# The second batch's layer norm placed ahead of GpSimd's masking in the second cross-attention, its query four units later, and zero products in TensorE's gaps

## What is computed

```
x = x + L0_xattn(layernorm(x), ctx)        # 16 heads of 64, softmax over 2048 keys
x = x + L0_attn(layernorm(x))              # latent attention with rope, causal, 16 heads of 8
x = x + L0_ffn(layernorm(x))               # 8 experts, the best one taken, gelu
x = x + L1_xattn(layernorm(x), ctx, mask)  # second cross-attention, 16 heads of 8
x = x + L1_attn(layernorm(x))              # one head of 128
x = x + L1_ffn(layernorm(x))               # 16 experts, 8 taken, and a shared one

L1_xattn: scores = (x Wq)(ctx Wk)^T / sqrt(8);  masked keys -> -1e32
          t = relu(scores + nbias)^2;  attn = t / (sum(t) + 1e-32);  (attn V) Wo
```

## Time and profile before

| | busy us | share of the span |
|---|---|---|
| TensorE (PE) | 430.9 | 89% |
| VectorE (DVE) | 343.6 | 71% |
| ScalarE (ACT) | 274.3 | 57% |
| GpSimd (POOL) | 165.3 | 34% |

### The profile page before, as it was taken

The page is one execution under the profiler, slowest core; times in us unless marked ns, Lnnn a source line. Parts: engine busy times, 40 slices in busy tenths (PEclk is TensorE's granted clock), DMA queues, the critical chain, the costliest instruction groups (busy, mean ns, idle before and its releaser), DMA issues.

```text
span 485.0 us, 8723 instructions
## 1 busy us (share of the span) xinstructions
PE 430.9 (89%) x3404; PEld 359.3 (74%) x3404; DVE 343.6 (71%) x538; ACT 274.3 (57%) x432; POOL 165.3 (34%) x108
## 2 busy tenths in 40 slices
PE   5897999999899999999878888699949999985896
PEld 3575899999799999999877745466437888864685
DVE  3478778878877888878631484761888999974574
ACT  2256667667567866667650235421019999982344
POOL 0012532334433633332536047300052657430024
PEclk9699899999899999999999899799959999999899
DMA  7613235332233323334359300089750000010000
GB/s 258 230 28 93 54 84 165 87 76 71 55 77 88 87 67 88 76 77 119 76 160 431 150 0 2 0 173 216 161 246 2 3 3 3 2 31 0 2 0 12
DMA packets 26984, 43.07 MB, mean 89 GB/s; under 512 B 5952, under 2 KB 24128, under 8 KB 25280
## 3 DMA queue, kind: packets, MB, share of 16 engines
q1 hardware_dynamic: 26944, 42.52, 31.3%
HBM read 19.30 MB, written 0.13 MB: 40 GB/s over the span
## 4 chain that ended last, share of the span: by engine, by line
PE 67%; DVE 15%; ACT 7%; issue 5%; SPq 2%; DMA 2%; POOL 1%; POOLq 0%; ACTq 0%; DVEq 0%
PE ps L561 6%; PE ps L563 6%; PE ps L562 6%; PE ps L583 5%; PE ps L585 5%; PE ps L584 5%; PE ps L577 5%; PE ps L832 4%; PE ps L855 3%; PE ps L932 3%; PE ps L789 3%; PE ps L797 3%; DVE max L1385 3%; DVE w_ring L1543 2%; SPq L449 2%
## 5 line engine op out<-in xcount | busy, mean ns | idle before, releaser
L1247 POOL TENSOR_TENSOR dT_lo<-z_sq,dT_hi 128x1024 fp32r<-128x1024 f32 x32 | 76.3, 2386 | 120.3 <-ACT dT_hi L961 120.3
L1385 DVE TENSOR_REDUCE max<-ps 128x1 f32<-128x1024 f32 x64 | 78.2, 1222 | 17.6 <-PE ps L563 14.5
L1543 DVE SCALAR_TENSOR_TENSOR w_ring<-ps,neg_nbias,cap 128x1024 f32<-128x1024 f32 x56 | 67.7, 1277 | 3.8 <-PE ps L832 3.3
L961 ACT ACTIVATE eT_hi<-ps 128x512 fp32r<-128x512 f32 x64 | 38.2, 597 | 54.4 <-PE ps L577 54.4
L561 PE MATMUL ps<-ctxT_hi,qk_hi 128*128 128x512 f32 x128 | 54.3, 425 | 8.7 <-ACT p_d L1030 7.3
L1180 ACT ACTIVATE p_ring<-w_ring,nbias_sb 128x1024 f32<-128x1024 f32 x56 | 61.6, 1145 | 0.6
L1372 DVE TENSOR_TENSOR eT_lo<-ps,eT_hi 128x512 fp32r<-128x512 f32 x64 | 43.9, 686 | 20.0 <-ACT eT_hi L961 19.9
L563 PE MATMUL ps<-ctxT_lo,qk_hi 128*128 128x512 f32 x128 | 52.4, 410 | 0.0
L562 PE MATMUL ps<-ctxT_hi,qk_lo 128*128 128x512 f32 x128 | 52.3, 409 | 0.0
L1381 DVE STREAM_TRANSPOSE y_sq<-p_d 128x1024 f32<-128x1024 f32 x32 | 39.9, 1245 | 16.8 <-ACT p_d L1030 15.9
L1030 ACT ACTIVATE p_d<-ps,nmax 128x1024 f32<-128x1024 f32 x32 | 35.7, 1115 | 27.2 <-DVE nmax L1415 27.2
(11 more groups left out here) (217 smaller groups left out, 891.9 us busy)
## 6 DMA issues: line engine op xcount, KB each, us to landing
z_sq<-y_sq SPq DMA_DIRECT2D x256, 64.0 KB, 2.1
w_sb<-in_w SPq DMA_DIRECT2D x2, 2048.0 KB, 14.4
kstack<-k_hi SPq DMA_DIRECT2D x8, 512.0 KB, 10.0
ctxT_raw<-in_ctx_t SPq DMA_DIRECT2D x2, 1024.0 KB, 7.3
ctx_raw<-in_ctx_nat SPq DMA_DIRECT2D x2, 1024.0 KB, 8.7
ctxT_raw<-in_ctx_t SPq DMA_DIRECT2D x1, 2048.0 KB, 7.7
kstack<-k_lo SPq DMA_DIRECT2D x4, 512.0 KB, 10.6
wg_sb<-in_wg SPq DMA_DIRECT2D x1, 1088.0 KB, 5.1
```

What stands on the lines that cost most here:

```text
L961: return nc.scalar.activation(dst, src, ACT.Copy)
L1247: nc.gpsimd.tensor_tensor(d_ring(dT_lo, m), z_chunk(m), d_ring(dT_hi, m), ALU.subtract)\
L1385: return v.tensor_reduce(max2[:, p:p + 1], ps[:, 2 * p:2 * p + 2, :], AX.XY, ALU.max)
L1543: v.scalar_tensor_tensor(w_ring[:, (at - 1) % 3, :].rearrange("p (h n) -> p h n", h=4), ps[:, bank:bank + 2, :].rearrange("p a (h n) -> p ...
```

## The change

Three things change.

1. Zero products are added: 4 ahead of `turn_xn(1)`, 2 inside it (between its transposes and its wait for the copy), 2 behind the latent product, 12 ahead of `turn_xn(2)`, 2 inside it, 4 behind `make_q1(0)`, and 6 behind the scores of units 2 and 3, where a wait for the copies of the first query stands ahead of them (they write its bank, 7).
2. `turn_xn(3)` moves from behind the last product of L797 to the middle of its last group of four. The first query goes to two banks (its first group to bank 3, the others to bank 7, by `q1_bank`), ScalarE copies the first group and signals it before the others are copied, and VectorE splits and spreads the first group as soon as it is there. `make_q1(0)` waits for `acc_zero`, since bank 7 is cleared by VectorE.
3. GpSimd waits for `xn_ready` of `layer_norm(4)` ahead of its loop. `turn_xn(4)` moves from m = 0 to m = 4 on TensorE, `make_q1(1)` from m = 2 to m = 6, ScalarE's copies likewise from m = 0 to m = 4 and m = 6 (each ahead of that unit's square), and VectorE's split of the second query from m = 4 to m = 9.

```diff
+        def q1_bank(b, g):
+            return 3 if b == 0 and g == 0 else 7
...
-            def turn_xn(i):
+            def turn_xn(i, bank=None):
                 pe.wait_ge(xn_ready, i + 1)
                 for b in range(*NORMS[i]):
                     last = nc.tensor.transpose(ps[:, XT_BANK[i], b * S:(b + 1) * S], xn[:, b, :], ident[:])
                 last.then_inc(xnT_psum, 1)
+                if bank is not None:
+                    keep_warm(bank, 2)
                 pe.wait_ge(xnT_ready, i + 1)
...
             fill(0)
-            turn_xn(1)
+            keep_warm(4, 4)
+            turn_xn(1, 4)
             pe.wait_ge(load["small"], 16 * N_SMALL)
             mm(ps[:, 5, T:2 * T], w_lat[:], xnT[:], start=True, stop=True).then_inc(lat_psum, 1)
+            keep_warm(4, 2)
...
             fill(3)
-            turn_xn(2)
+            keep_warm(4, 12)
+            turn_xn(2, 4)
...
                     for f in range(NF):
+                        if b and eh and f == NF // 2:
+                            turn_xn(3)
...
                 for g in range(4):
-                    last = mm(ps[:, 7 * b, g * S:(g + 1) * S], wq1[:, g, :], xnT[:, b * S:(b + 1) * S],
+                    last = mm(ps[:, q1_bank(b, g), g * S:(g + 1) * S], wq1[:, g, :], xnT[:, b * S:(b + 1) * S],
                               start=True, stop=True)
-                last.then_inc(q1_psum, 1)
+                    if g == 0 and b == 0 or g == 3:
+                        last.then_inc(q1_psum, 1)
             pe.wait_ge(load["wq1"], 16)
-            turn_xn(3)
+            pe.wait_ge(acc_zero, 1)
             make_q1(0)
+            keep_warm(2, 4)
...
                 if u == 1 and c == 1:
-                    pe.wait_ge(q1_done, 4)
+                    pe.wait_ge(q1_done, 6)
...
-                if m == 0:
+                if m == 2:
+                    pe.wait_ge(q1_done, 4)
+                    keep_warm(7, 6)
+                if m == 4:
                     turn_xn(4)
-                if m == 2:
+                if m == 6:
                     make_q1(1)
...
-            def copy_q1(b):
-                act.wait_ge(q1_psum, b + 1)
+            def copy_q1(b, g0_, g1_):
                 for t in (q1s, q1):
-                    nc.scalar.activation(t[:, :, b * S:(b + 1) * S], ps[:, 7 * b, :].rearrange("p (g s) -> p g s", g=4),
+                    nc.scalar.activation(t[:, g0_:g1_, b * S:(b + 1) * S],
+                                         ps[:, q1_bank(b, g0_), g0_ * S:g1_ * S].rearrange("p (g s) -> p g s", s=S),
                                          ACT.Copy, scale=SCALE1).then_inc(q1_done, 1)
-            copy_q1(0)
+            act.wait_ge(q1_psum, 1)
+            copy_q1(0, 0, 1)
+            act.wait_ge(q1_psum, 2)
+            copy_q1(0, 1, 4)
...
                     relu_first(0)
-                    copy_xnT(4)
-                    copy_q1(1)
...
+                if m == 4:
+                    copy_xnT(4)
+                if m == 6:
+                    act.wait_ge(q1_psum, 3)
+                    copy_q1(1, 0, 4)
...
             pool.wait_ge(keep_done, 1)
+            pool.wait_ge(xn_ready, 5)
...
             spread_q(v, 0).then_inc(qbd_done, 1)
+            dve.wait_ge(q1_done, 4)
             split_q1(0, slice(1, 4))
             layer_norm(4)
...
-                if m == UNITS // 2:
-                    dve.wait_ge(q1_done, 4)
+                if m == UNITS + 1:
+                    dve.wait_ge(q1_done, 6)
                     split_q1(1, slice(0, 4))
```

More of the change, by code:

```diff
@@ L508, in _, with keep_warm @@
             mm = nc.tensor.matmul
-            def turn_xn(i):
+            def keep_warm(bank, count):
+                for _ in range(count):
+                    mm(ps[:, bank, 0:T], zeros[:, 0:P], zeros[:], start=True, stop=True)
+            def turn_xn(i, bank=None):
                 pe.wait_ge(xn_ready, i + 1)
@@ L515, in turn_xn @@
                 last.then_inc(xnT_psum, 1)
+                if bank is not None:
+                    keep_warm(bank, 2)
                 pe.wait_ge(xnT_ready, i + 1)
-            def keep_warm(bank, count):
-                for _ in range(count):
-                    mm(ps[:, bank, 0:T], zeros[:, 0:P], zeros[:], start=True, stop=True)
             pe.wait_ge(warm, 1)
```

## The result

The changed kernel takes 485.56 us (median of 4 runs, 484.38 to 487.33) against 491.88 for the kernel before, measured beside it: ratio 0.9882, 95% interval 0.9835 to 0.9928. Two later measurements, each beside the kernel before, gave 0.9879 (0.9821 to 0.9938) and 0.9906 (0.9865 to 0.9946). The forecast was 488.1 us, a gain of 4.3 us. The profiled executions are closer together than the medians: 484.83 against 486.96 us. Each ratio is taken from fast runs alone: executions over 1.5% above the fastest of their kernel are left out of it.

The account below looks back on a forecast made before the run. Three engines are full at once in the second cross-attention's loop, so only its beginning has slack. The terms -0.5 + 0.8 - 4.6 (the last including 0.1 lost) gave -4.3, from 492.38 to 488.1 us, range 485.3 to 490.8.

Parts of the forecast that it names:

- A: Start of the latent attention: with zero products its instructions run at full clock and end at 277.2, 0.5 us gained.
- B: Twelve zero products ahead of `turn_xn(2)`: they outlast the norm, the transposes start at 311.0, 0.8 us lost.
- the lower bound (+0.3): Ahead of the experts: if the first `diag` takes its undisturbed 1.2 us, L780 starts at 316.0, 0.3 us late.
- C: The first query, around `turn_xn(3)`: scores start at 353.25 against 353.13, 0.1 us lost (bounds 0.4 gained, 0.6 lost).
- D: Start of the second cross-attention's loop: undisturbed `layer_norm(4)` and later second query bring combination 1's relu 4.6 us earlier.
- rival 1: Clock falls inside TensorE's new wait in `turn_xn(4)`: 489.7 us, chance 0.18; if it lasts until 367, 491.8 us.
- Catching up (2): In the loop, the shifted start removes the 0.3 us waits, up to 2.1 us more gained: 486.0 us, chance 0.08.
- The slow twelve (3): The twelve products ahead of `turn_xn(2)` run at half clock, experts start some 9 us late: 496 us; slower cases 0.08.
- Rival 4: `layer_norm(4)` is slowed by something other than GpSimd: about 1 us gained, 491.8 us; chance 0.13 together with a long fall.

Follow-up runs that it names:

- e3: The changed kernel without any of its added zero products, moves and GpSimd's wait kept: 486.52 us, ratio 0.9954 to the kernel before.
- e4: The changed kernel without its early zero products, those of the second cross-attention kept: 486.60 us, ratio 0.9943; again 485.56 us, 0.9891.
- the wait alone: The kernel before with GpSimd's wait for the norm as its only edit: 486.08 us, ratio 0.9940; again 486.11 us, 0.9903.

## Why the prediction was right

**What bounds.** Right. Three engines are full in the loop, and u to z is 62.59 to 63.10 in every profile of the table: the start of the loop alone moved its end.

**A.** 0.5 gained by forecast, 0.68 measured. In two later profiles without early zero products the half-clock stretch was missing all the same: there s to r is 8.89, and against those A loses 1.0. **B.** 0.8 lost, 0.72 measured. The transposes start at 311.00, the number forecast (`fill(3)` ended within 0.1 us of where it did before). The first `diag` started ahead of `k_lo`, so the lower bound (+0.3) applied to the first selection, 315.89 against 315.67. The other one came later by more. A and B cancel: s to e is 53.09 with them, 53.05 before, and 53.06 and 52.99 in the profiles of e3 and e4. In the second profiles of the wait alone and of e4 it is 53.52 and 53.58, so there the early products would be worth 0.5. What the forecast did not price is a smaller number of products: seven, with none inside `turn_xn(2)`, gain 1.15 us over none (41.32 against 42.47).

**C.** 0.1 forecast, 0.35 measured, within its bounds. Too small in it was the stop in the last group: VectorE's last part came 0.82 us later relative to the first expert product (351.02 - 321.08 against 349.38 - 320.26), not 0.57, and its splitting of the query starts right behind it, long after the early copy is there.

**D.** 4.6 forecast with C's 0.1 in it, so 4.7 from the first scores to the end of the loop; 3.6 measured (81.33 to 77.76). Of the four terms it is the furthest off. The walk was right to 0.3 us up to TensorE's wait (first `w_ring` 3.25 after the scores against 3.35, the wait 1.68 against 1.75), and there rival 1 came true: the clock was half from 363.2 to 366.6, which the prediction had also named as a sign of being wrong (half clock behind 360). Its price was 1.5 us (13.46 against 14.99), 1.6 in the rival. Without the fall D is 5.1, 0.4 over the forecast. Of the three profiles of the changed kernel the clock fell in two, and of all six with this loop in four; what decides it isn't shown. The Trainium skill, TensorE: Matmul & The Clock Gate, section Why this matters for your kernels, asks that gaps stay under about 3 us. That was not enough here: the gap was 1.7 us.

The forecast tied D too closely to the clock: with TensorE at half clock as before it left 1 us of gain. The wait alone, at half clock for 10 us, gained 3.5 us of q to u, and for 17 us still 1.55. The falls in the kernel before were also read late: by the earlier trace rows they came at 308.1 and 352.4, not at 308.5 and 352.7, so the idling ahead of the second was 1.7 us.

**The sum.** In the profiled executions the gain is 2.1 us: the stages s to z give 3.2, and 0.8 was lost ahead of s and 0.2 behind z, in code that did not change. In the runs the ratios of the three measurements come to 5.8, 6.0 and 4.6 us (each times the median of before, as 0.0118 x 491.88). So the size forecast, 4.3, is a little low against the runs and high against the first profile. The mechanism was right; that the number came out inside the range is in part luck. Taken from 492.38, the stages' 3.2 us would give 489.2 us, near what rival 1 said (489.7). The 485.56 measured lies below that and only 0.3 us above the lower end of the range. No stage explains it; the third measurement, with the most runs of before, is closest to the stages. What in the executions of before adds the difference in the other two is open.

**Rivals.** Catching up (2) did not happen: a combination takes 8.78 us (relu to relu, mean of six) against 8.76, and the waits of 0.2 to 0.4 us are all there. The slow twelve (3) did not: by the microsecond view the clock was full from 269 to 347. Rival 4 is refuted by the norm's 2.87 us.

## What to carry to other kernels

Where a stage has three full engines, as this loop has, look at its first few microseconds for what stands ahead of the bottleneck's first instruction in its own program order: there was all that this change could win. Keep a chain of small VectorE instructions clear of long GpSimd ones with SBUF inputs; one wait on the engine with slack was, by the medians, the whole gain. Size zero products to end with what TensorE waits for, since each one behind that delays the work that waits, and judge them by the stage and not by the mean clock. Take more than one profile of each kernel before calling a part worthless: two executions of the same kernel differed here by 3 us in the stages that were compared.

## What the runs showed of the hardware

The spread of one kernel's executions goes with its mean granted clock. Of the kernel before on one chip, those with 0.958 to 0.965 took 484.3 to 488.1 us, those with 0.953 to 0.955 took 487.2 to 491.3. The places differ from one execution to the next: a half-clock stretch at 273 to 277 in the kernel before cost s to r 1.7 us (10.58), and in the second profile of the wait alone, which is the same code there, it was missing (8.89) and 2.2 us came back in r to e (44.63). The second profile without early zero products shows the same two numbers (8.89 and 44.69). In the profiles with the early zero products this variation is missing (s to r is always 9.90, r to e 43.18 or 43.19 with twelve and 41.32 or 41.33 with seven). The mean clock is higher with the added products, 0.968 to 0.982 in the changed kernel against 0.947 to 0.972 in the wait alone on the same chip, while the medians are level (485.78 against 486.11 us).
